# One core, AdaLN with a Mamba-2 block: the order of masks and products on VectorE, of decays and exp(A) on ScalarE, and what TensorE's waits for an output bank name

## The reference

```python
proj = jnp.einsum('bsd,ed->bse', x, in_proj_w)           # gate, hBC, dt
hBC  = silu(causal depthwise conv of 4 taps over hBC, plus bias)  # -> hs, Bm, Cm
L = jnp.exp(_segsum(A_dt))                               # decays within a chunk
Y_diag = jnp.einsum('bzlhn,bzshn,bhzls,bzshp->bzlhp', Cc, Bc, L, xch)
states = jnp.einsum('bzlhn,bhzl,bzlhp->bzhpn', Bc, decay_states, xch)
Y_off = jnp.einsum('bzlhn,bzhpn,bhzl->bzlhp', Cc, prev, jnp.exp(A_cum))
Y = (Y_diag + Y_off).reshape(b, s, H, P) + hs * D[None, None, :, None]
g = y * jax.nn.silu(gate)
gg = gg * jax.lax.rsqrt(mean(gg * gg over the group's 1024 channels) + EPS)
return jnp.einsum('bsi,oi->bso', out, out_proj_w)
```

## Time and profile before

| | |
|---|---|
| median of 3 runs | 1873.5 us (1872.71 to 1877.07) |
| the profiled execution | 1870.3 us |
| its span, first to last instruction | 1868.5 us |
| mean granted clock of PE | 0.988 |
| PE busy | 1754.7 us, 94% |
| DVE busy | 1290.5 us, 69% |
| ACT busy | 1065.5 us, 57% |
| POOL busy | 942.1 us, 50% |

### The profile page before, as it was taken

One profiled execution on the slowest core, in us unless ns is written; L12 is line 12 of the kernel. 1 busy time (PEld: TensorE's weight loads), 2 busy tenths in 40 slices (PEclk: granted clock), 3 DMA queues, 4 the chain that ended last, 5 costly groups with the idle time before them and its releaser, 6 DMA issues.

```text
span 1868.5 us, 31134 instructions
## 1 busy us (share of the span) xinstructions
PE 1754.7 (94%) x9656; PEld 1344.0 (72%) x9656; DVE 1290.5 (69%) x2095; ACT 1065.5 (57%) x1946; POOL 942.1 (50%) x721
## 2 busy tenths in 40 slices
PE   6799999999999999999999999999999999999966
PEld 5567777777777777777777777777777777777755
DVE  5766667666766677766676667666777666766788
ACT  6566555656646565665546566465656555565632
POOL 2355453556535464554535555355644545455563
PEclk9899999999999999999999999999999999999988
DMA  6412121111202121121211212121211212111121
GB/s 224 130 30 69 55 66 44 50 60 57 66 28 72 49 66 51 35 66 55 66 45 48 62 54 68 29 72 45 70 51 29 72 55 66 44 48 61 34 96 57
DMA packets 77097, 114.14 MB, mean 61 GB/s; under 512 B 21376, under 2 KB 28032, under 8 KB 76032
## 3 DMA queue, kind: packets, MB, share of 16 engines
q1 hardware_dynamic: 59360, 80.06, 14.2%
q10 hardware_dynamic: 17568, 31.99, 5.1%
HBM read 88.94 MB, written 23.07 MB: 60 GB/s over the span
## 4 chain that ended last, share of the span: by engine, by line
issue 46%; POOL 34%; PE 9%; DVE 5%; ACT 3%; DMA 1%; SPq 1%; POOLq 1%; ACTq 0%; DVEq 0%
POOL yt L1605 9%; POOL ssq L1600 7%; POOL wg_lo L1524 4%; POOL wo_lo L1524 4%; POOL prev L1586 3%; POOL yt L1608 3%; POOL wx_lo L1524 3%; PE bank L476 2%; PE bank L478 2%; PE bank L477 2%; PE bank L641 1%; PE bank L706 1%; DMA raw_w<-w_in_dram 1%; PE bank L840 1%; ACT lm L1072 0%
## 5 line engine op out<-in xcount | busy, mean ns | idle before, releaser
L1605 POOL TENSOR_TENSOR yt<-yt,ea 128x384 f32<-128x384 f32 (+1 forms) x128 | 189.6, 1481 | 393.1 <-DVE ea L1440 393.1
L1218 DVE SCALAR_TENSOR_TENSOR xc<-bank,bpar,xc 128x511 f32<-128x511 f32 (+2 forms) x384 | 285.4, 743 | 52.8 <-ACT xc L906 48.3
L1410 DVE TENSOR_TENSOR lm<-lm,cbm 128x512 f32<-128x512 f32 x256 | 185.9, 767 | 155.7 <-ACT lm L1075 155.7
L476 PE MATMUL bank<-h_hi,wg_hi 128*128 128x512 f32 x640 | 262.0, 409 | 31.3 <-ACT gate L1030 21.9
L478 PE MATMUL bank<-h_hi,wg_lo 128*128 128x512 f32 x640 | 251.0, 392 | 0.0
L477 PE MATMUL bank<-h_lo,wg_hi 128*128 128x512 f32 x640 | 250.2, 391 | 0.0
L476 PE MATMUL bank<-wo_hi,g_hi 128*128 128x512 f32 x496 | 206.9, 417 | 7.2 <-POOL wo_lo L1524 7.2
L476 PE MATMUL bank<-h_hi,wx_hi 128*128 128x512 f32 x512 | 210.3, 411 | 2.2 <-DVE bt L1218 2.2
L1586 POOL TENSOR_TENSOR prev<-prev,dec 128x512 f32<-128x512 f32 x96 | 102.0, 1063 | 206.0 <-DVE prev L1356 131.9
L478 PE MATMUL bank<-h_hi,wx_lo 128*128 128x512 f32 x512 | 200.3, 391 | 0.0
L477 PE MATMUL bank<-h_lo,wx_hi 128*128 128x512 f32 x512 | 199.9, 390 | 0.0
(11 more groups left out here) (187 smaller groups left out, 3796.9 us busy)
## 6 DMA issues: line engine op xcount, KB each, us to landing
raw_w<-w_in_dram SPq DMA_DIRECT2D x145, 256.0 KB, 2.6
raw_w<-w_out_dram SPq DMA_DIRECT2D x64, 256.0 KB, 2.6
part_d<-part ACTq DMA_DIRECT2D x64, 256.0 KB, 2.0
part<-part_d ACTq DMA_DIRECT2D x58, 256.0 KB, 2.7
rt<-rows_d SPq DMA_DIRECT2D x256, 8.0 KB
acc<-x_dram SPq DMA_DIRECT2D x8, 256.0 KB, 6.6
acc<-w_mod_dram SPq DMA_DIRECT2D x2, 1024.0 KB, 6.0
lh<-neg_d SPq DMA_DIRECT2D x128, 8.0 KB
```

Source lines behind the costliest of these rows:

```text
L476: nc.tensor.matmul(out_ap, whi(k), hhi(k), start=(k == 0), stop=False)
L1218: stt(dst[:, at], ps[:, 0:HALF - 3 + k], w(k), dst[:, at], ALU.mult, ALU.add)\
L1410: tt(lm[:, h % 4, :], lm[:, h % 4, :], cbm[:, toks(hf)], ALU.mult).then_inc(v_m, 1)
L1605: tt(yt[:, j % 2, cols], yt[:, j % 2, cols], ea[:, j % 2, cols], ALU.add).then_inc(p_t3, 1)
```

## The change

Three orders change and one kind of wait.

On DVE, the two masks of step j + 1 are made after the two products of step j, not before. On ACT, the decays of a step are made ahead of the copy of exp(A). On PE, a wait for `v_acc` (the sum is in `acc`) at an output bank becomes a wait for what reads the bank: `v_accin` in units c = 0 and 3, where the read is an operation of its own, and the copy's `v_acc` in the others; this applies to the output products z = 2 and 3, to exp_a(1) and to the diagonal product of step 0. In the last unit PE waits for the first copy of exp(A) before it writes the gate rows.

```diff
+            def out_read(g, c, z):
+
+                u = UPG * g + c
+                if c in (0, 3):
+                    te.wait_ge(v_accin, 8 * (g - 1 if c == 0 else g) + (4 if c == 0 else 0) + z + 1)
+                else:
+                    ge(te, v_acc, 4 * (u - 1) + z + 1)
+
-            def out_proj(u, z, b=None):
+            def out_proj(u, z, b=None, gc=None):
...
-                if z >= 2 and b is None:
+                if gc and b is None and z >= 2:
+                    out_read(*gc, z - 2)
+                elif z >= 2 and b is None:
                     te.wait_ge(v_acc, 4 * u + z - 1)
...
                     elif j == 1:
-                        ge(te, v_acc, 4 * (u - 1) + (1 if end else 3))
+                        if not first:
+                            out_read(g, c, 0 if end else 2)
...
-                            out_proj(u - 1, 2)
+                            out_proj(u - 1, 2, None, (g, c))
...
-                        out_proj(u - 1, z)
+                        out_proj(u - 1, z, None, (g, c))
...
                     if j == 0:
-                        if not end:
-                            ge(te, v_acc, 4 * u)
+                        if not end and not first:
+                            out_read(g, c, 3)
...
                         te.wait_ge(a_gate, 4 * UNITS)
+                        te.wait_ge(a_ea, 4 * (UNITS - 1) + 1)
...
                 act(warm[:, :], mhalf[:, 0:1], ACT.Exp)
+                decays(0)
                 exp_a(0)
-                decays(0)
...
                     if j < NCT - 1:
+                        decays(j + 1)
                         exp_a(j + 1)
-                        decays(j + 1)
...
                 for j in range(NCT):
-                    if j < NCT - 1:
-                        mix(2 * j + 2)
-                        mix(2 * j + 3)
-
                     ve.wait_ge(t_yd, 4 * u + j + 1)
...
                     tt(ea[:, j % 2, cols], bank[6][:, cols], ea[:, j % 2, cols], ALU.mult).then_inc(v_t1, 1)
+                    if j < NCT - 1:
+                        mix(2 * j + 2)
+                        mix(2 * j + 3)
                     if j >= 1:
                         lower_g(j - 1)
```

## The result

| | time, median | times | ratio to before, 95% interval |
|---|---|---|---|
| before | 1873.1 us (4 runs) | 1869.15 to 1877.07 | 1 |
| after | 1917.1 us (4 runs) | 1914.84 to 1919.33 | 1.0235 [1.021, 1.026] |

The change makes the kernel 44 us slower; 61 us slower was predicted (1934.5 us). The profiled execution of after took 1919.33 us, its span is 1917.4 us, the mean granted clock of PE 0.981 (before 0.988). In the code of after L1410 is L1422, L1417 is L1429, L1435 is L1443, L1440 is L1448, L1218 is L1230, L792 is L803, L779 is L790, L706 is L717, ACT's L1075 is L1087; POOL's L1605, L1608 and L1524 are L1616, L1619 and L1535; the gate read L1030 is L1042.

The account below looks back on a forecast made before the run. PE, busy in 94% of the span, was taken as the bound, idling mainly at unit ends. Unit boundaries +38.4 and +32, the bank wait -10.5 and the tail +1 gave +61 us: 1934.5 us, range 1856 to 1957.

Parts of the forecast that it names:

- step 0: First step of a unit on DVE: its extra 1.1 us is hidden by the wait for a projection.
- Part 3: DVE's masks behind both products meet POOL's work on SBUF; masks and g_lo are held up, making the kernel slower.
- Part 1: PE's wait for the bank's read instead of the sum into acc: 1.5 us saved seven times, -10.5 us.
- c = 0 to 1: End of unit c = 0: DVE's longer steps make PE's output product late, +1.8 us in each of 8 groups.
- c = 1 to 2: End of unit c = 1: DVE's longer steps make PE's transposes late, +2.3 us in each of 8 groups.
- c = 2 to 3: End of unit c = 2: the least hurt, one mask being slow already; +0.7 us in each of 8 groups.
- c = 3 to the next group: DVE's full list delays PE's next gate product: +4.8 us in five groups, +4 in two.
- last unit and tail: Later DVE steps cost up to 2.5 us each, a 3.1 us PE stall goes: +1 us, bounds -2 and +4.
- Part 2: ACT's copies of exp(A) come later, behind the decays, but nothing waits for them: cost 0.
- Lower first: Rival, chance 0.14: DVE's g_lo gets the port before POOL's gate product; -14 us, 1859.5 us.
- No new contention: Rival, chance 0.14: DVE's masks do not meet POOL, products come 1.2 us earlier; some 36 us gained, 1837 us.

Follow-up runs that it names:

- dve_only: The kernel before with DVE's new order alone, masks behind the two products: 1932.1 us, ratio 1.032.
- lower_first: The changed kernel with DVE's g_lo put ahead of the two masks, behind both products: 1947.8 us, ratio 1.0408.
- no_dve: The changed kernel with DVE's old order, so PE's new waits and ACT's new order together: 1843.1 us, ratio 0.9841.
- by_unit: The changed kernel with masks between DVE's two products in units c = 0 to 2 and ahead of both in c = 3: 1839.8 us, ratio 0.9825.
- pe_only: The kernel before with PE's new waits alone: 1862.0 us, ratio 0.9941.
- act_only: The kernel before with ACT's new order, decays ahead of the copy of exp(A), and the last unit's extra wait: 1855.6 us, ratio 0.9906.

## Why the prediction was right, and where its sum was off

**Sign, cause and place** were right: masks in pairs behind ea(j) meet POOL's sum, mask b and `g_lo` are held up in turn, step 0 hides it, and steps 1 and 2 pay. The marks that it named are there: the masks' mean is 1050 ns (over 1000), mask b takes 1.78 us in half 1 (1.51 in half 0, not 1.8), `g_lo` 1.76 (near 1.9), and PE's wait for `acc` is replaced by one for `xc`. Waits for `ea`, which it expected too, did not grow (7.7 us before, 4.5 after). The 17 us too many come from these terms.

**Part 3, DVE's order: 71.4 us forecast, 58 measured alone.** The profiled span of dve_only is 60 us above before's, and the block sums show where. Each row goes from yd(0) of a unit to yd(0) of the next; the wait at yd(0) of c = 3, Part 1's place, has a row of its own:

| boundary | forecast | dve_only | after |
|---|---|---|---|
| c = 0 to 1 | +14.4 | +8.3 | +8.2 |
| c = 1 to 2 | +18.4 | +20.1 | +17.5 |
| c = 2 to 3 | +5.6 | -0.6 | -0.7 |
| the wait at yd(0) of c = 3 | -10.5 | +0.8 | -11.2 |
| c = 3 to the next group | +32 | +33.1 | +33.4 |
| last unit and tail | +1 | -0.4 | +2.3 |

*The step was mis-sized.* The prediction gave DVE 5.55 + 2.44 = 7.99 us from yt(1) to yt(2) in half 1 and 5.13 + 2.32 = 7.45 in half 0. After takes 848.51 - 840.85 = 7.66 and, in c = 0, 7.07. The convolution starts 5.24 us behind yt(1), not 5.55. The miss is in the hand-overs: I let the blocked instruction end 0.55 us (0.58) behind POOL's and began the next from that end. The 0.55 is right (mask b ends at 844.49, the sum at 843.94), but the next instruction starts some 0.1 us before the end shown, twice on DVE, and POOL's turn is shorter than its 1.25 by as much. Two steps in each of four units are 2 x (0.38 + 0.33 + 0.38 + 0.33) = 2.84 us a group, some 22 us over the boundaries of the table, where the step is the bound. At c = 0 to 1 and c = 2 to 3 (2 x 0.38 x 8 = 6.1 us each) this is the entire miss: 14.4 - 6.1 = 8.3 and 5.6 - 6.1 = -0.5.

*A term was missing that hid more than half of this:* PE's clock behind its new waits. After the 2.41 us wait above, the matmuls of L477 and L478 take 0.63 us each and not 0.39. The windows of the same stretch (busy us of PE, PEld, DVE, ACT, POOL, then the granted clock and DMA):

```profile
852.00:856.00 4.00, 1.88 (x24) 1.51 (x22) 4.00 (x8) 1.87 (x3) 4.00 (x3) 1.00 0.00 0
856.00:858.00 2.00, 1.71 (x4) 1.43 (x5) 2.00 (x4) 1.08 (x2) 0.60 (x2) 0.57 0.35 126
858.00:860.00 2.00, 2.00 (x6) 1.57 (x6) 2.00 (x7) 1.74 (x4) 1.92 (x2) 0.57 0.02 5
860.00:862.00 2.00, 2.00 (x10) 1.63 (x9) 1.12 (x2) 1.31 (x3) 2.00 (x3) 1.00 0.00 0
```

The granted clock was 0.57 of full over these 4 us: it fell to its lower level (1.2 GHz) for some 3 us. Eight steps between the 24 matmuls are 0.1 to 0.3 us longer, which makes the transposes 1.5 us late: with all at 0.23 us from start to start, the 24 would have ended the stretch at 861.9, which is where the prediction's chain from yt(3) (856.16 + 5.85 = 862.0) ends too. Such matmuls can be counted: those of L476 to L478 that waited for nothing and yet start more than 0.36 us behind the one before (0.23 is usual). Up to the last unit's yd(3) they lost 9.1 us in after, 14.4 in dve_only and 20.8 in lower_first; before, no_dve and by_unit have none. At c = 1 to 2 the loss is 7.5 us in dve_only and 4.5 in after, and with it the boundary comes out: 18.4 - 5.3 (two steps of half 1) + 7.5 = 20.6 for 20.1 measured, and 18.4 - 5.3 + 4.5 = 17.6 for 17.5. At c = 3 of dve_only, 32 - 4.6 + 6.9 = 34.3, for 33.1. So Part 3 alone is about 71 - 22 + 14 = 63, for 60 in the span and 58 in the medians. That the forecast missed by no more is in part luck: two errors of opposite sign.

**Part 1, the wait for the bank's read: -10.5 forecast, -12.5 alone.** By the block sums 8.0 of it is at yd(0) in c = 3 of pe_only, and 11.2 in after, where the decays come earlier as well; that is the -7 (1.05 x 7 = 7.3) and -10.5 of the prediction. The interval of pe_only, -8.4 to -13.5 us, takes in the whole forecast and its bound of -11.0.

**Part 2, ACT's order: 0 forecast, -18.9 alone, but about -3 here.** dve_only to after is PE's and ACT's parts on top of the new DVE order: -15 us, of which PE's is some 12; the -3 left is within the noise. By the block sums the two spans differ by 12 us at yd(0) of c = 3 and by 3 at c = 1 to 2, where the clock fell less often, and after gives 3 back in the last unit and tail. For the change as a whole the 0 did little harm. As a statement on ACT's order it was wrong, since it asked only who waits for the copy, and not who waits for the decays: in before the masks did, 121 times and 155.7 us in all, and yt(j) behind them.

**The sum.** Terms 58 - 15 = +43 (44 measured) for 71.4 + 0 - 10.5 = 61. 13 us of the 17 are Part 3's, the rest Parts 1 and 2.

**The rivals.** Lower first did not come about by an order of arrival: mask b was blocked, then the gate product went, and `g_lo` waited, as the row of the 1.79 us mask said. Put there by hand it costs 31 us more, not less. No new contention was priced at 1837; with POOL's operations made short the price of the order does vanish, and the kernel whose masks avoid POOL by their place takes 1840 us. That rival was thus a fair price for another change, though not for its own reason alone: the old order with PE's and ACT's parts takes 1843.

What stays open: in the last unit and tail after is 2.7 us worse than dve_only, and at c = 3 to the next group it is no better, although the clock cost it less there. The chain of silus and gate reads that follows is entered at another moment in each kernel, and PE's waits for ACT's gate differ with it (12.3 us in dve_only, 17.0 in after). No run parts that.

## What to carry to other kernels

Before moving a two-operand SBUF instruction of DVE, look at what its neighbour releases on POOL: the instruction that starts POOL should be followed on DVE by work with a PSUM operand, or by one instruction with two SBUF operands at most, and masks like these belong ahead of it (ahead of both products or between them made no difference that the runs tell). A wait that is "hidden" on one order may be the bound on another (ACT's order gave 19 us beside one DVE order and about 3, within the noise, beside the other), so the parts of a change are to be priced in the order in which they will run together. Where a change gives PE new waits of the sizes seen here (1.1 to 2.5 us), put a term for the clock into the sum.

## What the runs showed of the hardware

- **DVE and POOL take turns.** With both queues full of instructions with two SBUF operands, each instruction goes through after one of the other engine's, so 0.68 us of DVE becomes 1.78 and 1.28 of POOL 1.60 to 1.73 (step 1 above; 95 of 96 second masks and all 62 `g_lo` of steps 1 and 2 in after). The Trainium skill, "SBUF — State Buffer", section "Who interferes with whom", calls the shared port pair an exclusive lock and has the loser block fully; the trace agrees (1.78 us for 0.68, 1.76 for 0.74). DVE's next instruction starts 0.47 us after POOL's has ended in the record (844.41 against 843.94), so a full turn of both took 1.70 us (842.71 to 844.41), less than 0.68 + 1.28.
- **Waits of PE of 1.1 to 2.5 us were followed by the lower clock, in some groups and not in others.** At c = 1 to 2 of after the same 2.41 to 2.50 us stood ahead of gate products in all 8 groups, and the slow matmuls followed in 3 of them (in 5 of 8 in dve_only). In lower_first PE waits 2.07 us for masks in c = 0 and 2, and the granted clock fell to 0.5 behind 11 of the 16. At a group's third gate product of after it fell behind 1.94, 2.21 and 2.38 us. At the waits of 1.66 us of c = 0 to 1 it never did; but in c = 3 it fell at a wait of 1.11 us for `lm` that followed two of 0.65 us (once in after, twice in dve_only), so the length of the last wait alone does not tell.
- **Idle time where the hardware loop jumps.** At the end of c = 3, ahead of the next group's gate products, PE idled up to 1.7 us in 4 groups of after for nothing that the profile shows, and ACT 2.47 us ahead of a gate read (group 3):

```profile
971.13 0.49 PE L476 MATMUL bank<-h_hi,wg_hi 128*128 128x512 f32 x1 [1.36 <-issue]
```

```profile
980.98 0.60 ACT L1042 ACTIVATE gate<-bank 128x512 f32<-128x512 f32 x1 [2.47 <-issue]
```

In before ACT has this too (2.21 us), but PE's "issue" between 110 and 1700 us is only 0.8 us in all. It is 4.7 in pe_only, 5.4 in dve_only, 5.9 in after, 6.9 in no_dve and 3.2 in by_unit, but 0.5 in act_only and none in lower_first. It follows neither PE's program nor DVE's alone, and its cause is open.
